# A transformer stack on one core: the rotation layer's QR and sign LU moved from TensorE and VectorE to row steps on GpSimd

## The chip, the cores and the metric

The kernel runs on one core of a Trainium2 chip. The metric is device time in microseconds for one launch, the median of three runs. The engines are named as in the profile: PE is TensorE (PEld its weight loads), DVE is VectorE, ACT is ScalarE, POOL is GpSimd, and SP is the queue that issues most DMAs. Each engine works through its own instructions strictly in the order of the program; semaphores tie the engines together.

## What is computed

Two images of 512 tokens with 144 channels pass through three transformer layers, each of 16 heads of width 9 with attention and an MLP of width 576 (layer 0 has four experts, two chosen per token). A last layer rotates the channels. Its matrices come from the weights and the condition alone:

```python
def _rotation(cond, W, b):
    v = jax.nn.silu(cond) @ W.T + b              # W: 2016 x 144
    A = zeros((2, 64, 64)); A[upper] = v; A[lower] = -v
    return expm(A)
U, _ = jnp.linalg.qr(P)                          # P: 144 x 64
R = _rotation(cond, W, b)
z = x @ U
x_rot = x + (z @ R - z) @ U.T
```

So beside the layers there is a solver: the entries v, the exponential of a 64 x 64 skew matrix for each image, and a QR of P, whose signs are fixed by an LU without pivoting of the upper 64 x 64 square of Q.

## The kernel before, in words

The layers run as 6 blocks (layer by image). A block is 64 steps, one for each head and each 128 keys; a step computes a tile of scores on PE, its exponential on ACT, and the row maxima of a later head (PE into one of three PSUM banks m_bank, then a reduce to row_max on DVE). Everything else is woven between the 384 steps: norms, the next block's q, k, v, the output projection, gates and MLPs of the block before. Which step a piece stands in comes from a table worked out when the kernel is built, and every engine walks the same table, each issuing its own part. POOL's parts are the norm's scale and shift (h_tok, L589 to L593), the low halves of q and k (L607, L609), and the split of each weight matrix into high and low halves (prep, L559 to L566, three layers and twelve MLPs). SP loads item after item of weights: one load waits until POOL has split the item before it.

The solver has three chains in the same table. The v chain takes steps 1 to 33 on DVE (L1051) and ends with a store to a DRAM scratch, from which SP fills the skew matrix with 63 small DMAs (L490). The exponential takes steps 141 to 257. The QR chain is the one that changes: 64 rounds "mgs" (modified Gram-Schmidt) and 64 rounds "lu". One round of either: PE spreads row j over 64 partitions by a matmul with a column of the identity (L1466, into an m_bank), DVE computes a coefficient for each row, and DVE adds the scaled row to all later rows (mgs: L1066 to L1079; lu: L1092 to L1101). 15 rounds lie in the head, before step 0; the others follow every two and a half steps, up to step 285, where signs, then y and m, make the final matrices.

```python
for i, part in enumerate(QR_CHAIN[EARLY:]):
    plan[i * QR_PACE // 2].append(part)
```

Of the kernel before, what the change touches and what calls it, by code (L numbers as in the profile page):

```python
# [26 lines left out]
ALU = mybir.AluOpType  # L27
# [4 lines left out]
P = 128  # L32
# [34 lines left out]
WCH = 2  # L67
# [79 lines left out]
QR_CHAIN = [("p_load",)] + [("mgs", j) for j in range(S)] + [("unit_cols",)]  # L147
QR_CHAIN += [("lu", j) for j in range(S)] + [("signs",), ("less_one",), ("y",), ("m", 0), ("m", 1)]
# [5 lines left out]
HEAD_SLOTS = sum(len(BANKS_OF[st[0]]) for st in HEAD)  # L154
EARLY = HEAD_SLOTS - HEAD_FROM + T * GRP // 2
QR_PACE = 5
# [20 lines left out]
def head_parts(slot):  # L177

    return QR_CHAIN[slot - HEAD_FROM:slot - HEAD_FROM + 1] if slot >= HEAD_FROM else []


def first_parts(i):

    at = HEAD_SLOTS - HEAD_FROM + i // 2
    return QR_CHAIN[at:at + 1] if i % 2 else []

SOLVER_BANK = ("v_rows", "p_load", "mgs", "lu", "skew", "taylor", "turned", "square", "y", "m")
# [46 lines left out]
def build(nc, a, out):  # L236
    with ExitStack() as ctx:
# [6 lines left out]
        def sem(name):  # L244
# [64 lines left out]
        w_rows = sb("w_rows", [VP, 2, WCH, C])  # L309
# [7 lines left out]
        bc_row = sb("bc_row", [S, C])  # L317
        bc_sq = sb("bc_sq", [S, C])
# [37 lines left out]
        w_in = [sem(f"w_in{i}") for i in range(2)]  # L356
# [7 lines left out]
                 "dve_done pool_done solver_full col_done v_summed "  # L364
# [65 lines left out]
        def _(sp):  # L430
# [17 lines left out]
            def load_w(i):  # L448
                if i >= 2:
                    sp.wait_ge(s["v_summed"], WCH * (i - 1))  # L450
                sp.dma_start(w_rows[:, i % 2, :, :],
                             a["L3_cond_W"].rearrange("(t p) c -> p t c", p=VP)[:, WCH * i:WCH * (i + 1), :])\
                    .then_inc(w_in[i % 2], 16)
# [22 lines left out]
            load_w(1)  # L476
            load_ada(1)
            load_item(1)
            for i in range(2, VT // WCH):
                load_w(i)  # L480
            load_item(2)
            load_item(3)

            sp.wait_ge(scratch_in, 16)
            sp.wait_ge(s["consts_ready"], 1)
            flat = v_scratch.rearrange("(b t) p -> b (t p)", b=B)
            off = 0
# [19 lines left out]
        def _(pool):  # L507
# [142 lines left out]
        def _(act):  # L650
# [87 lines left out]
            def solver(step):  # L738
# [19 lines left out]
            for i in range(T * GRP):  # L758
                mring.take()
                for part in first_parts(i):  # L760
                    solver(part)
# [24 lines left out]
        def _(dve):  # L786
# [248 lines left out]
            def solver(step, taken):  # L1035
# [10 lines left out]
                if kind == "v":  # L1046
                    t = step[1]
                    i = t // WCH
                    dve.wait_ge(w_in[i % 2], 16 * (i // 2 + 1))
                    for b in range(B):  # L1050
                        ins = dve.tensor_tensor_reduce(out=bc_scr[0:VP, :], in0=w_rows[:, i % 2, t % WCH, :],  # L1051
# [10 lines left out]
                elif kind == "mgs":  # L1062
                    j = step[1]
                    row = bk[0:S, 0:C]
                    dve.wait_ge(s["solver_full"], full)
                    link(dve.tensor_copy(bc_row[:, :], row))  # L1066
                    dve.tensor_tensor_reduce(out=bc_sq[:, :], in0=bc_row[:, :], in1=bc_row[:, :], scale=1.0, scalar=0.0,
                                             op0=ALU.mult, op1=ALU.add, accum_out=s_small[:, 3:4])\
                        .then_inc(s["dve_done"], 1)
                    dve.tensor_tensor_reduce(out=bc_scr[0:S, :], in0=q_rows[:, :], in1=bc_row[:, :], scale=1.0,  # L1070
                                             scalar=0.0, op0=ALU.mult, op1=ALU.add, accum_out=s_small[:, 0:1])\
                        .then_inc(s["dve_done"], 1)
                    done[0] += 2
                    fill[0]()
                    dve.wait_ge(s["dve_done"], done[0])
                    link(dve.reciprocal(s_small[:, 1:2], s_small[:, 3:4]))
                    link(dve.tensor_scalar(s_small[:, 2:3], s_small[:, 0:1], s_small[:, 1:2], neg_after[:, j:j + 1],
                                           ALU.mult, ALU.mult))
                    drain(dve.scalar_tensor_tensor(out=q_rows[:, :], in0=bc_row[:, :], scalar=s_small[:, 2:3],  # L1079
                                                   in1=q_rows[:, :], op0=ALU.mult, op1=ALU.add))  # L1080
                elif kind == "unit_cols":
                    link(dve.tensor_tensor_reduce(out=bc_scr[0:S, :], in0=q_rows[:, :], in1=q_rows[:, :], scale=1.0,
                                                  scalar=0.0, op0=ALU.mult, op1=ALU.add,
                                                  accum_out=s_small[:, 0:1]))
                    rsqrt(s_small[:, 1:2], s_small[:, 0:1], s_small[:, 2:3])
                    link(dve.tensor_scalar(q_rows[:, :], q_rows[:, :], s_small[:, 1:2], None, ALU.mult))
                    dve.tensor_copy(lu[:, :], q_rows[:, 0:S]).then_inc(s["col_done"], 1)
                elif kind == "lu":
                    j = step[1]
                    dve.wait_ge(s["solver_full"], full)  # L1090
                    w = bk[0:S, j:j + 1]
                    link(dve.tensor_scalar(s_sign[:, j:j + 1], w, 0.0, 2.0, ALU.is_ge, ALU.mult))  # L1092
# [89 lines left out]
            for i in range(T * GRP):  # L1182
                take_max(0, *divmod(i, GRP))
                for part in first_parts(i):
                    solve(part)
# [37 lines left out]
        def _(pe):  # L1223
# [221 lines left out]
            def solver(step):  # L1445
# [9 lines left out]
                elif kind == "p_load":  # L1455
                    pe.wait_ge(p_in, 64)
                    pe.transpose(bk[0:S, 0:P], p_nat[:, :], ident[:, :])
                    ins = pe.transpose(bk[0:S, P:C], p_nat_d[:, :], ident[0:CR, 0:CR])
                elif kind in ("mgs", "lu"):
                    j = step[1]  # L1460
                    src = q_rows[:, :] if kind == "mgs" else lu[:, :]
                    if kind == "lu" and j == 0:
                        pe.wait_ge(s["col_done"], 1)
                    else:
                        pe.wait_ge(*last[chain])
                    ins = pe.matmul(bk[0:S, 0:src.shape[1]], ident[0:S, j:j + 1].to_broadcast([S, S]), src,  # L1466
                                    start=True, stop=True)
# [48 lines left out]
            for i in range(T * GRP):  # L1516
                max_scores(0, *divmod(i, GRP))
                for part in first_parts(i):
                    solver(part)
# [40 lines left out]
```

## Time and profile before

| | us |
|---|---|
| median of 3 runs (lowest, highest) | 1165.92 (1162.24, 1166.27) |
| span of the profiled execution | 1173.7 |
| PE busy in it | 948.9 (81%) |
| DVE busy in it | 713.6 (61%) |
| ACT busy in it | 412.4 (35%) |
| POOL busy in it | 198.5 (17%) |

The profile is of one execution; the time of that execution is its span, 7.8 us above the median of the runs. Busy time counts work alone; an engine that waits for a semaphore is idle. Lines such as L1466 are lines of the kernel before. A line of a group of instructions has the shape "line engine operation out<-in, shapes, xcount | busy us, mean ns | idle us just before them and what ended it".

### The profile page before, as it was taken

Reading aid. Unit: us, or ns where it says so; the run is one execution under the profiler, and the core shown is the slowest. Engines: PE = TensorE matmul, PEld = TensorE weight load, DVE = VectorE, ACT = ScalarE, POOL = GpSimd, SP = SyncE. Lnnn points to the kernel's source line nnn. Section 1 sums busy time; section 2 is a strip of 40 time slices with the busy share of each in tenths; the row PEclk is TensorE's granted clock in tenths of the full one; section 3 lists DMA queues with packets and bytes.
Section 4 is the critical chain, followed back from the end, with each engine's and each line's share of the span. In section 5 each row is a group of like instructions: output and inputs, shape, how many; then the busy total and the mean of one; then the engine's idle time right before and its main releaser. Section 6 shows DMA issues by size and latency. Waiting matters only on the chain.

```text
span 1173.7 us, 12067 instructions
## 1 busy us (share of the span) xinstructions
PE 948.9 (81%) x3791; PEld 513.7 (44%) x3791; DVE 713.6 (61%) x2140; ACT 412.4 (35%) x742; POOL 198.5 (17%) x350
## 2 busy tenths in 40 slices
PE   4666889877898768889877788778887978989847
PEld 1432443335765433357644434535433534335326
DVE  4388767775353887772457767656677365564333
ACT  0302342324341333343424432415332436435412
POOL 5201014010240110042420000311002211012020
PEclk9999755556775655566866555657555656558556
DMA  3000001010111000001110000100000100000000
GB/s 101 13 1 10 16 6 43 1 29 1 29 29 29 17 1 1 1 16 42 34 38 0 1 1 1 29 1 1 1 1 0 30 0 1 1 1 1 6 5 11
DMA packets 22025, 16.01 MB, mean 14 GB/s; under 512 B 6427, under 2 KB 19391, under 8 KB 21962
## 3 DMA queue, kind: packets, MB, share of 16 engines
q1 hardware_dynamic: 21914, 15.22, 4.8%
q8 instruction: 31, 0.51, 0.2%
q14 instruction: 32, 0.26, 0.1%
q10 hardware_dynamic: 48, 0.02, 0.0%
HBM read 14.62 MB, written 0.61 MB: 13 GB/s over the span
## 4 chain that ended last, share of the span: by engine, by line
PE 61%; DVE 29%; issue 4%; ACT 4%; POOL 2%; DMA 0%; DVEq 0%; SPq 0%; ACTq 0%; POOLq 0%
PE o_bank L1289 11%; PE m_bank L1268 11%; DVE row_max L823 7%; PE s_bank L1257 3%; PE m_bank L1466 3%; PE d_bank L1350 3%; PE d_bank L1407 2%; PE d_bank L1409 2%; PE d_bank L1408 2%; PE m_bank L1276 2%; PE d_bank L1306 2%; PE d_bank L1307 2%; PE d_bank L1239 2%; PE d_bank L1392 2%; PE d_bank L1321 2%
## 5 line engine op out<-in xcount | busy, mean ns | idle before, releaser
L663 ACT ACTIVATE probs<-s_bank 128x512 f32<-128x512 f32 x384 | 220.4, 596 | 546.6 <-PE s_bank L1257 544.0
L823 DVE TENSOR_REDUCE row_max<-m_bank 128x1 fp32r<-128x512 f32 x384 | 256.0, 686 | 151.9 <-PE m_bank L1268 147.1
L1268 PE MATMUL m_bank<-k_t,q_t 32*128 32x512 f32 x384 | 216.5, 752 | 61.9 <-DVE q_rows L1079 24.2
L1257 PE MATMUL s_bank<-q_t,k_t 32*128 32x512 f32 x384 | 239.4, 749 | 5.8 <-ACT probs L663 4.9
L1289 PE MATMUL o_bank<-probs,v_aug 128*32 128x512 f32 x768 | 178.2, 1019 | 3.9 <-DVE o_tok L841 3.2
L1268 PEld LDWEIGHTS m_bank<-k_t,q_t 32*128 32x128 f32 x384 | 81.6, 271 | 181.9 <-issue 62.9
L1257 PEld LDWEIGHTS s_bank<-q_t,k_t 32*128 32x128 f32 x384 | 90.6, 272 | 30.9 <-ACT probs L663 16.1
L589 POOL TENSOR_TENSOR h_tok<-h_tok,mod 128x144 f32<-128x144 f32 x48 | 24.0, 499 | 297.3 <-DVE h_tok L882 297.3
L1407 PE MATMUL d_bank<-ff_hi,g_hi 128*128 128x144 f32 x192 | 60.7, 316 | 1.5 <-ACT g_hi L733 1.4
L1409 PE MATMUL d_bank<-ff_lo,g_hi 128*128 128x144 f32 x192 | 60.7, 316 | 0.0
L1408 PE MATMUL d_bank<-ff_hi,g_lo 128*128 128x144 f32 x192 | 60.5, 315 | 0.0
L1466 PE MATMUL m_bank<-q_rows,ident 64*64 64x144 f32 x128 | 45.9, 460 | 16.8 <-DVE q_rows L1079 16.8
L982 DVE TENSOR_TENSOR g_lo<-g_raw,g_hi 128x512 fp32r<-128x512 f32 x48 | 37.3, 787 | 34.1 <-ACT g_hi L733 33.9
L1321 PE MATMUL d_bank<-ident,h_tok 128*128 128x128 f32 x80 | 35.0, 439 | 19.4 <-POOL h_tok L593 19.4
L607 POOL TENSOR_TENSOR qs_tok<-qkv_tok,qs_tok 128x144 fp32r<-128x144 f32 x24 | 12.0, 500 | 222.9 <-ACT ks_tok L712 222.9
L1276 PEld LDWEIGHTS m_bank<-ident_r,row_max 128*128 128x128 f32 x96 | 22.3, 323 | 62.3 <-issue 39.0
L592 POOL COPY h_tok<-o_tok 128x144 f32<-128x144 f32 x24 | 7.4, 307 | 245.0 <-DVE o_tok L841 215.2
L1392 PE MATMUL d_bank<-h_hi,ff_hi 128*128 128x512 f32 x60 | 33.1, 552 | 19.1 <-ACT g_hi L733 12.6
L731 ACT ACTIVATE g_raw<-d_bank 128x512 f32<-128x512 f32 x60 | 36.0, 600 | 31.2 <-PE d_bank L1395 23.9
L1407 PEld LDWEIGHTS d_bank<-ff_hi,g_hi 128*128 128x128 f32 x192 | 44.1, 230 | 4.9 <-ACT g_hi L733 4.9
L1276 PE MATMUL m_bank<-ident_r,row_max 128*128 128x128 f32 x96 | 26.6, 429 | 24.1 <-DVE q_rows L1079 9.1
L1409 PEld LDWEIGHTS d_bank<-ff_lo,g_hi 128*128 128x128 f32 x192 | 44.7, 233 | 0.0
(232 smaller groups left out, 1639.4 us busy)
## 6 DMA issues: line engine op xcount, KB each, us to landing
raw_a<-in_L_cond_w_dram SPq DMA_DIRECT2D x20, 288.0 KB
raw_a<-in_L_cond_W_fc_dram SPq DMA_DIRECT2D x4, 288.0 KB
w_rows<-in_L_cond_W_dram SPq DMA_DIRECT2D x8, 141.8 KB
raw_d<-in_L_cond_w_dram SPq DMA_DIRECT2D x30, 36.0 KB
raw_a<-in_L_cond_w_dram SPq DMA_DIRECT2D x20, 36.0 KB
x_tok<-in_x_dram SPq DMA_DIRECT2D x2, 288.0 KB, 4.2
out_dram<-moe SPq DMA_DIRECT2D x4, 144.0 KB, 1.9
raw_d<-in_L_cond_w_dram SPq DMA_DIRECT2D x30, 4.0 KB
```

The costliest lines, as they stand in the source:

```text
L663: act.activation(probs[:, n % PROBS, :], s_banks[n % S_BANKS][:, :], ACT.Exp, scale=HD ** -0.5)\
L823: dve.tensor_reduce(row_max[:, grp % 2, t, MAXROW + 32 * j:MAXROW + 32 * j + 1], bk[:, :], AX.X, ALU.max).then_inc(drained, 1)
L1257: pe.matmul(s_banks[n % S_BANKS][:, :], k_t[rows, par, g, kt * P:(kt + 1) * P], q_t[rows, par, g, :], start=True, stop=True).then_inc(s["s ...
L1268: pe.matmul(bk[:, :], q_t[rows, par, g, t * P:(t + 1) * P], k_t[rows, par, g, :], start=True, stop=True).then_inc(s["max_full"], 1)
L1276: ins = pe.matmul(bk[:, t * P:(t + 1) * P], row_max[:, grp % 2, t, :], ident_r[:, :], start=True, stop=True)
L1289: ins = pe.matmul(o_bank[32 * j:32 * j + 32, :], v_aug[:, par, kt, at:at + 32], probs[:, (GRP * quad + j) % PROBS, :], start=(kt == 0), st ...
L1321: pe.transpose(a_bank[:, cols], h_tok[:, t, 0:P], ident[:, :])
L1392: pe.matmul(bk[:, :], ff_hi[:, i, c], h_hi[:, :], start=True, stop=False)
L1407: pe.matmul(dst, g_hi[:, f, cols], ff_hi[:, i, w], start=(f == 0), stop=False)
L1408: pe.matmul(dst, g_lo[:, f, cols], ff_hi[:, i, w], start=False, stop=False)
L1409: pe.matmul(dst, g_hi[:, f, cols], ff_lo[:, i, w], start=False, stop=False)
L1466: ins = pe.matmul(bk[0:S, 0:src.shape[1]], ident[0:S, j:j + 1].to_broadcast([S, S]), src, start=True, stop=True)
```

## The change

The QR becomes an elimination on the Gram matrix: the head computes P'P and the transposed P side by side as one tile aug of 64 x 208, and 63 rounds "gs" on POOL clear it row by row; the 64 lu rounds go to POOL too. In each round SP sends the pivot row to all 64 partitions by a DMA from SBUF to SBUF (row_out), and POOL waits for it, works out the coefficient (the reciprocal is a power of minus one), scales the row and adds it. A round stands at every second step from step 0 on; the rounds in the head are gone. Since SP now sends rows, its whole list is written along the steps: rows, weight items, the four loads of the v chain (of four tiles each, into a single buffer where two of two tiles took turns) and the 63 skew DMAs each stand where their step is. DVE waits for all 63 gs at step 126 (unit_cols) and for the last lu at step 256 (signs).

```diff
-WCH = 2
+WCH = 4
-QR_PACE = 5
+QR_PACE = 2
-    for i, part in enumerate(QR_CHAIN[EARLY:]):
-        plan[i * QR_PACE // 2].append(part)
+    for i, part in enumerate(QR_CHAIN):
+        plan[i * QR_PACE].append(part)
...
+            def row_out(k):
+                kind, j = SWEEPS[k]
+                if k == 0:
+                    sp.wait_ge(m_drained[0], 1)
+                elif k == S - 1:
+                    sp.wait_ge(s["col_done"], 1)
+                else:
+                    sp.wait_ge(s["swept"], k)
+                src = (aug if kind == "gs" else lu)[j:j + 1, j:]
+                w = src.shape[1]
+                sp.dma_start(row_bc[:, j:j + w], src.unsqueeze(1).to_broadcast([1, S, w]))\
+                    .then_inc(row_in, 16)
...
+            for n in range(BLOCKS * STEPS):
+                for i in range(2, ITEMS):
+                    if PREP_AT[i - 1] == n:
+                        load_item(i)
+                for part in SOLVER_PLAN[n]:
+                    if part[0] == "v" and part[1] % WCH == WCH - 1 and part[1] < VT - 1:
+                        load_w(part[1] // WCH + 1)
+                    if part in SWEEPS and part != SWEEPS[-1]:
+                        row_out(SWEEPS.index(part) + 1)
+                    if part[0] == "v_rows":
+                        sp.wait_ge(scratch_in, 16)
...
+                pool.wait_ge(row_in, 16 * (k + 1))
+                if step[0] == "gs":
+                    link(pool.tensor_tensor(inv, row, minus_one[:, :], ALU.pow))
+                    link(pool.tensor_scalar(coef, rows[:, j:j + 1], inv, after, ALU.mult, ALU.mult))
+                else:
+                    link(pool.tensor_scalar(s_sign[:, j:j + 1], row, 0.0, 2.0, ALU.is_ge, ALU.mult))
...
+                    link(pool.tensor_scalar(piv, s_sign[:, j:j + 1], -1.0, row, ALU.add, ALU.add))
+                    link(pool.tensor_tensor(sq, piv, piv, ALU.mult))
+                    link(pool.tensor_tensor(inv, sq, minus_one[:, :], ALU.pow))
+                    link(pool.tensor_scalar(inv, inv, piv, after, ALU.mult, ALU.mult))
+                    link(pool.tensor_scalar(coef, rows[:, j:j + 1], inv, None, ALU.mult))
+                link(pool.tensor_scalar(row_bc[:, rest], row_bc[:, rest], coef, None, ALU.mult))
+                pool.tensor_tensor(rows[:, rest], rows[:, rest], row_bc[:, rest], ALU.add).then_inc(s["swept"], 1)
```

Three places of the order matter below. The first is SP where the v chain ends. Before, the skew DMAs (L490) followed the loads of weight items 2 and 3 in SP's list:

```order
L437 DMA raw_a<-in_L_cond_w_proj_dram 128x144
L437 DMA raw_d<-in_L_cond_w_proj_dram 16x144 x3
L437 DMA raw_d<-in_L_cond_b_proj_dram 1x144 x2
L490 DMA skew<-v_scratch 1x2x63 [waits consts_ready,scratch_in]
L490 DMA skew<-v_scratch 1x2x62
L490 DMA skew<-v_scratch 1x2x61
```

Now, on SP, they stand (as L522) behind the DMA of row 17, which is the row of 191 columns (a row of gs(j) has 208 - j columns):

```order
L477 DMA row_bc<-aug 64x1x193 [waits swept]
L477 DMA row_bc<-aug 64x1x192 [waits swept]
L477 DMA row_bc<-aug 64x1x191 [waits swept]
L522 DMA skew<-v_scratch 1x2x63 [waits consts_ready,scratch_in]
L522 DMA skew<-v_scratch 1x2x62
L522 DMA skew<-v_scratch 1x2x61
```

Behind the last of the 63, still on SP, come rows 18 to 22 and the load of weight item 2, which waits for POOL's split of item 1:

```order
L522 DMA skew<-v_scratch 1x2x2
L522 DMA skew<-v_scratch 1x2x1
L477 DMA row_bc<-aug 64x1x190 [waits swept]
L477 DMA row_bc<-aug 64x1x189 [waits swept]
L477 DMA row_bc<-aug 64x1x188 [waits swept]
L477 DMA row_bc<-aug 64x1x187 [waits swept]
L477 DMA row_bc<-aug 64x1x186 [waits swept]
L448 DMA raw_a<-in_L_cond_w_dram 128x576 [waits weights_ready]
```

So all 63 skew DMAs now lie between rows 17 and 18, and the items lie behind row 22. The second place is POOL before its norm of block 0 (h_tok from o_tok). Before, the three splits (ff for items 1 and 2, lay for item 3) followed the last low half of k directly:

```order
L609 TENSOR_TENSOR ks_tok<-qkv_tok,ks_tok 128x16x9
L559 CAST ff_hi<-raw_a 128x1360 [waits item_in]
L560 TENSOR_TENSOR ff_lo<-raw_a,ff_hi 128x1360 [waits pool_done]
L564 CAST ff_d<-raw_d 96x784
L566 TENSOR_TENSOR ff_d<-raw_d,ff_d 32x784 [waits pool_done]
L559 CAST ff_hi<-raw_a 128x1360 [waits item_in,weights_ready]
L560 TENSOR_TENSOR ff_lo<-raw_a,ff_hi 128x1360 [waits pool_done]
```

Now POOL has gs rounds in front of them (this is gs(20), gs(21) and the split of item 1):

```order
L665 TENSOR_TENSOR pivot<-row_bc,minus_one 64x1 [waits row_in]
L666 TENSOR_SCALAR pivot<-aug,pivot,neg_after 64x1 [waits pool_done]
L677 TENSOR_SCALAR row_bc<-row_bc,pivot 64x187 [waits pool_done]
L678 TENSOR_TENSOR aug<-aug,row_bc 64x187 [waits pool_done]
L665 TENSOR_TENSOR pivot<-row_bc,minus_one 64x1 [waits row_in]
L666 TENSOR_SCALAR pivot<-aug,pivot,neg_after 64x1 [waits pool_done]
L677 TENSOR_SCALAR row_bc<-row_bc,pivot 64x186 [waits pool_done]
L678 TENSOR_TENSOR aug<-aug,row_bc 64x186 [waits pool_done]
L589 CAST ff_hi<-raw_a 128x1360 [waits item_in]
```

Each split and each h_tok now stands behind every gs round of an earlier step. The third place is PE in the steps of block 0, where before a solver matmul (L1466) stood between scores and maxima and waited for banks that DVE empties:

```order
L1268 MATMUL m_bank<-k_t,q_t 128x512 [waits m_drained2]
L1257 MATMUL s_bank<-q_t,k_t 128x512 [waits probs_ready]
L1466 MATMUL m_bank<-q_rows,ident 64x144 [waits m_drained0]
L1268 MATMUL m_bank<-k_t,q_t 128x512 [waits m_drained1]
L1257 MATMUL s_bank<-q_t,k_t 128x512 [waits probs_ready]
```

Now, on PE, only the maxima (L1283) use these banks there, beside the scores (L1272) and o_bank:

```order
L1283 MATMUL m_bank<-k_t,q_t 128x512 [waits m_drained0]
L1272 MATMUL s_bank<-q_t,k_t 128x512 [waits probs_ready]
L1304 MATMUL o_bank<-probs,v_aug 32x512 [waits probs_ready]
L1304 MATMUL o_bank<-probs,v_aug 32x512 x3
L1283 MATMUL m_bank<-k_t,q_t 128x512 [waits m_drained1]
L1272 MATMUL s_bank<-q_t,k_t 128x512 [waits probs_ready]
```

The 128 solver matmuls are gone from PE, and with them their turns in the ring of three banks.

## Rows read from the trace of the kernel before

**Rows 1.** The page: the chain that ended last, shares of the span.

```profile
PE 61%; DVE 29%; issue 4%; ACT 4%; POOL 2%; DMA 0%; DVEq 0%; SPq 0%; ACTq 0%; POOLq 0%
```

**Rows 2.** Groups by line on PE: the solver's matmul and the maxima behind it.

```profile
L1268 PE MATMUL m_bank<-k_t,q_t 32*128 32x512 f32 x384 | 216.5, 752 | 61.9 <-DVE q_rows L1079 24.2 <-DVE lu L1101 16.5 <-DVE row_max L823 14.6
...
L1466 PE MATMUL m_bank<-q_rows,ident 64*64 64x144 f32 x128 | 45.9, 460 | 16.8 <-DVE q_rows L1079 16.8
```

**Rows 3.** Timeline of DVE before step 0 (start, length): pairs of maxima, four rounds apart.

```profile
63.13 1.29 DVE L823 TENSOR_REDUCE row_max<-m_bank 128x1 fp32r<-128x512 f32 x2
...
75.06 1.29 DVE L823 TENSOR_REDUCE row_max<-m_bank 128x1 fp32r<-128x512 f32 x2
```

**Rows 4.** Timeline of POOL: starts of h_tok, image 1, then block 0.

```profile
94.85 0.53 POOL L589 TENSOR_TENSOR h_tok<-h_tok,mod 128x144 f32<-128x144 f32 x1 [36.38 <-DVE h_tok L882]
...
238.14 0.30 POOL L592 COPY h_tok<-o_tok 128x144 f32<-128x144 f32 x1 [29.87 <-issue]
```

**Rows 5.** Groups by line on POOL: two long operations, two short ones.

```profile
L560 POOL TENSOR_TENSOR ff_lo<-raw_a,ff_hi 128x1360 fp32r<-128x1360 f32 x12 | 37.3, 3106 | 7.8 <-issue 6.9
...
L590 POOL TENSOR_TENSOR h_tok<-h_tok,mod 128x144 f32<-128x144 f32 x48 | 23.7, 494 | 3.8
...
L593 POOL COPY h_tok<-h_tok 128x32 f32<-128x32 f32 x80 | 16.7, 213 | 50.2 <-DVE h_tok L880 45.7
L559 POOL CAST ff_hi<-raw_a 128x1360 fp32r<-128x1360 f32 x12 | 16.0, 1330 | 112.3 <-PE d_bank L1417 103.9 <-DMA raw_d<-in_L_cond_b_dram 8.4
```

**Rows 6.** DMA issues: KB each, then us from issue to landing.

```profile
x_tok<-in_x_dram SPq DMA_DIRECT2D x2, 288.0 KB, 4.2
...
c_row<-in_cond_dram SPq DMA_DIRECT2D x1, 144.0 KB, 3.1
...
p_nat_d<-in_L_cond_P_dram SPq DMA_DIRECT2D x1, 4.0 KB, 1.6
qk_gain<-in_L_cond_g_q_dram SPq DMA_DIRECT2D x1, 4.5 KB, 2.3
qk_gain<-in_L_cond_g_k_dram SPq DMA_DIRECT2D x1, 4.5 KB, 2.6
...
v_scratch<-v_row ACTq DMA_DIRECT2D x1, 15.8 KB, 1.4
```

**Rows 7.** Timeline of POOL: splits of items 1 (start) and 3 (start, last operation).

```profile
173.75 1.39 POOL L559 CAST ff_hi<-raw_a 128x1360 fp32r<-128x1360 f32 x1
...
204.04 0.66 POOL L559 CAST lay_hi<-raw_a 128x576 fp32r<-128x576 f32 x1 [7.32 <-DMA raw_d<-in_L_cond_b_proj_dram]
...
206.87 1.40 POOL L566 TENSOR_TENSOR lay_d<-raw_d,lay_d 32x576 fp32r<-32x576 f32 x1
```

**Rows 8.** Timeline of SP: first issue of item 3, then the skew DMAs.

```profile
196.75 0.35 SPq L437 DMA_DIRECT2D raw_a<-in_L_cond_w_qkv_dram  x1
...
201.94 36.63 SPq L490 DMA_DIRECT2D skew<-v_scratch  x63
```

**Rows 9.** Busy time of L1466 by stretch: stretch, length, PE and PEld busy (count), clock, DMA.

```profile
238.00:387.00 149.00, 7.81 (x22) 3.04 (x22) 0.64 0.10 26
387.00:478.00 91.00, 8.90 (x28) 3.89 (x28) 0.54 0.00 1
478.00:611.00 133.00, 4.28 (x20) 2.55 (x20) 0.68 0.11 29
611.00:709.00 98.00, 7.38 (x32) 4.46 (x32) 0.53 0.00 1
709.00:787.00 78.00, 3.59 (x16) 2.18 (x16) 0.59 0.04 11
787.00:879.00 92.00, 7.08 (x34) 4.35 (x34) 0.59 0.00 1
879.00:1173.70 294.70, 4.29 (x20) 2.57 (x18) 0.60 0.02 5
```

**Rows 10.** Groups by line on PE from 879.00 us to the end.

```profile
L1466 PE MATMUL m_bank<-lu,ident 64*64 64x64 f32 x20 | 4.6, 334 | 11.1 <-DVE lu L1101 11.1
```

More of the change, by code:

```diff
@@ L146 @@
 V_CHAIN = [("v", t) for t in range(VT)] + [("v_rows",)]
-QR_CHAIN = [("p_load",)] + [("mgs", j) for j in range(S)] + [("unit_cols",)]
-QR_CHAIN += [("lu", j) for j in range(S)] + [("signs",), ("less_one",), ("y",), ("m", 0), ("m", 1)]
+SWEEPS = [("gs", j) for j in range(S - 1)] + [("lu", j) for j in range(S)]
+QR_CHAIN = SWEEPS[:S - 1] + [("unit_cols",)] + SWEEPS[S - 1:]
+QR_CHAIN += [("signs",), ("less_one",), ("y",), ("m", 0), ("m", 1)]
 EXP_CHAIN = [("skew",), ("scale",)] + [("taylor", n) for n in range(TAYLOR - 1, 0, -1)] + [("turned",)]
@@ L177, in head_parts, with prep_steps @@
 def head_parts(slot):
[L179 to L189, printed above, removed]
+    return [("p_load",)] if slot == HEAD_FROM else []
+def prep_steps():
+    at, slots = {}, [n for n in range(BLOCKS * STEPS) for _ in range(SLOTS[n])] + [BLOCKS * STEPS] * 8
+    slot = 0
+    for st in WOVEN:
+        if st[0] == "prep":
+            at[st[1]] = slots[slot]
+        if st[0] == "mlp" and 1 <= st[1] < MLPS - 1:
+            at[mlp_item(st[1] + 1)] = slots[slot]
+        slot += len(ROOM[st[0]])
+    return at
+PREP_AT = prep_steps()
+SOLVER_BANK = ("v_rows", "p_load", "skew", "taylor", "turned", "square", "y", "m")
 MAX_SHARE = [2, 2] + [1] * (GSTEPS - 4) + [0, 0]
@@ L307, in build @@
         ident_r = sb("ident_r", [P, P], F32R)
-        w_rows = sb("w_rows", [VP, 2, WCH, C])
+        w_rows = sb("w_rows", [VP, WCH, C])
         v_col = sb("v_col", [VP, B, VT])
@@ L355, in build @@
         p_in = sem("p_in")
-        w_in = [sem(f"w_in{i}") for i in range(2)]
+        w_in = sem("w_in")
+        row_in = sem("row_in")
         scratch_in = sem("scratch_in")
@@ L626, in solver @@
                     pool.partition_all_reduce(rs_norm[:, 1, :], rs_norm[:, 0, :], S, RMAX).then_inc(s["norm_out"], 1)
+                if step not in SWEEPS:
+                    return
+                j, k = step[1], SWEEPS.index(step)
+                row, rest = row_bc[:, j:j + 1], slice(j + 1, (S + C) if step[0] == "gs" else S)
+                rows, after = (aug if step[0] == "gs" else lu), neg_after[:, j:j + 1]
+                piv, inv, coef, sq = (pivot[:, i:i + 1] for i in range(4))
+                pool.wait_ge(row_in, 16 * (k + 1))
[4 more added lines that the diff above has]
+                    link(pool.tensor_scalar(s_sign[:, j:j + 1], row, 0.0, 2.0, ALU.is_ge, ALU.mult))
+                    if j == S - 1:
+                        pool.tensor_copy(lu[:, j:j + 1], row).then_inc(s["swept"], 1)
+                        return
+                    link(pool.tensor_scalar(piv, s_sign[:, j:j + 1], -1.0, row, ALU.add, ALU.add))
[5 more added lines that the diff above has]
+                pool.tensor_tensor(rows[:, rest], rows[:, rest], row_bc[:, rest], ALU.add).then_inc(s["swept"], 1)
             walk = {"norm": norm, "qkv": qkv, "mlp": mlp}
@@ L1061, in solver @@
                     dve.tensor_tensor(v_row[:, :], bk[0:B * VT, 0:VP], vb_row[:, :], ALU.add).then_inc(drained, 1)
[L1062 to L1080, printed above, removed]
@@ L1456, in solver @@
                     pe.wait_ge(p_in, 64)
[L1457 to L1467, printed above, removed]
+                    pe.matmul(bk[0:S, 0:S], p_nat[:, :], p_nat[:, :], start=True, stop=False)
+                    pe.matmul(bk[0:S, 0:S], p_nat_d[:, :], p_nat_d[:, :], start=False, stop=True)
+                    pe.transpose(bk[0:S, S:S + P], p_nat[:, :], ident[:, :])
+                    ins = pe.transpose(bk[0:S, S + P:S + C], p_nat_d[:, :], ident[0:CR, 0:CR])
                 elif kind == "skew":
```

85 lines of the change are left out of this document (30 added, 55 removed).

## The prediction

> **What bounds the kernel now.** I read first the chain of the work that ended last, [rows 1]: 61% of the span is PE, 29% DVE, and POOL 2%. The groups by line then say what the QR has to do with that. A maxima matmul (L1268) waited 24.2 us for a DVE that was finishing an mgs round and 16.5 us for one finishing a lu round, and the solver's own matmul (L1466) 16.8 us for the round before it [rows 2]: 57.5 us in which PE stood still for the QR, beside its busy time, which the stretches give as 43.3 us after 238 us [rows 9]. So the QR does lie on the path. The timeline of POOL shows the other side: an engine that waits most of the time, but whose norms PE waits for. 238.1 us is where h_tok of block 0 begins [rows 4], and POOL had been idle 29.87 us before it.
>
> **What the change removes.** Ahead of step 0, eight mgs rounds stood between the maxima. Two pairs of maxima four rounds apart are 11.93 us apart [rows 3], 2.98 for a round with its maxima; without the round the pair of maxima takes 1.29. That saves 1.69 a round, 13.5 us for eight. The seven rounds in the head I count at nothing: they lie between loads and turns, and 7 x 1.69 = 11.8 us is the most that they can hold. After 238 us I credit L1466's busy time in each stretch [rows 9], and the 11.1 us that it waited in the last stretch [rows 10] by half (5.6), since a DVE that was behind there may be behind with other work. The other waits on DVE's rounds stay out of the sum; they are the unknown on the side of a gain.
>
> **What a round costs now.** The trace has no such operation on POOL, so I fit two lines to [rows 5]. Two inputs: (3106 - 494) / (1360 - 144) = 2.15 ns a column, 185 ns at no width. One input: (1330 - 213) / (1360 - 32) = 0.84 ns, 186 ns at no width. L590 shows 3.8 / 48 = 0.08 us between dependent operations. A gs round has four: pow and coefficient on one column (an estimate of 0.25 each; 0.19 is the lower bound, 0.5 for pow alone my upper one), the scaled row, some 190 wide, 0.35, the addition 0.59, gaps 0.32: 1.8 us. A lu round has eight, narrower: five at 0.19, pow 0.25, 0.21, 0.25, gaps 0.64: 2.3 us.
>
> The row's DMA is the disputed price. No DMA of the trace has SBUF at both ends. The nearest [rows 6]: plain 4 KB 1.6 us, a store out of SBUF 1.4, 4.5 KB spread over 128 partitions 2.3 and 2.6, 144 KB spread likewise 3.1. For gs I take the mean of 1.6, 2.3, 2.6 and 3.1, 2.4 us; for the shorter lu rows that of the first three, 2.2; bounds 1.6 and 3.1. With 0.1 us from POOL's semaphore to SP (an estimate) a gs round takes 1.8 + 0.1 + 2.4 = **4.3 us**, a lu round 2.3 + 0.1 + 2.2 = **4.6**. Nothing overlaps within a round: row k+1 leaves only when sweep k is over.
>
> **Stage A, to h_tok of block 0.** Image 1's h_tok is twelve operations of 0.53, 0.494 and 0.213 (four of each), 5.0 us, from 94.85 [rows 4, 5]; gs(0) begins at 94.85 + 5.0 - 13.5 = 86.4 us. gs(16) is over at 86.4 + 16 x 4.3 + 1.8 = 157.0. Three rows (those behind rows 4, 8 and 12) queue behind a load of w_rows; x_tok, of the same size, took 4.2 us [rows 6], so each is late by 4.2 - 2.4 = 1.8, together 5.4: 162.4. Row 17 leaves, and now SP issues the 63 skew DMAs: 36.6 us in the trace of before [rows 8], where nothing waited behind them but weights. Now rows 18 and on do: 199.0, and row 18 is there at 201.5. (The v chain itself should be done by then; its last loads go with row 12, at some 142.) gs(18) to gs(21): 3 x 4.3 + 1.8, 216.2. Then POOL splits items 1 and 2, with the load between them, which before took from 173.75 to the first issue of item 3 at 196.75 [rows 7, 8], 23.0: 239.2. SP issues item 3, 201.94 - 196.75 = 5.2: 244.4; row 23 lands 2.5 later, 246.9. gs(23) to gs(33), 10 x 4.3 + 1.8: 291.7. The split of item 3, 208.27 - 204.04 = 4.2 [rows 7]: 295.9. Only then h_tok of block 0 comes, for which PE waits in step 70: **57.8 us later** than 238.1. DVE and ACT reach that step early and wait too, so what was saved before the step is lost there.
>
> **Stages after it** [rows 9]. In each stretch the longer of two paths decides: PE's (the stretch less L1466), or POOL's (h_tok 5.0, then its rounds one behind the other).
> 238 to 387: four rounds fit into what the weights leave; -7.8, lag 50.0.
> 387 to 478: POOL 5.0 + 15 x 4.3 + 3 (unit_cols on DVE, an estimate) + 2 x 4.6 = 81.7, PE 91 - 8.9 = 82.1; -8.9, 41.1.
> 478 to 611: -4.3, 36.8.
> 611 to 709: POOL 5.0 + 19 x 4.6 = 92.4, above PE's 90.6; 98 before, -5.6, 31.2.
> 709 to 787: -3.6, 27.6.
> 787 to 879: POOL 92.4 + 3 for the signs on DVE = 95.4 against 92; +3.4, 31.0.
> To the end: -4.3 - 5.6, 21.1.
> The profiled execution took 1173.7, so its counterpart takes 1194.8; the median lies 7.8 below such an execution: **1187 us**, 1.8% slower.
>
> **Rivals.** Half a per cent, 6 us, is about what a measurement of this kernel can tell.
>
> *The row lands as a plain small load (faster).* At 1.6 us (the 4 KB load and the store speak for it, and that the broadcasts stood among many loads [rows 6]) a gs round takes 3.5 and a lu round 4.0. Stage A: 86.4 + 16 x 3.5 + 1.8 + 3 x 2.6 = 152.0; + 36.6 + 1.7 = 190.3; + 10.5 + 1.8 + 23.0 + 5.2 + 1.7 = 232.5; + 35 + 1.8 + 4.2 = 273.5, a lag of 35.4. POOL then holds nobody up in the later stretches, and all of L1466 and its last wait come back: 43.3 + 11.1 = 54.4. 1173.7 + 35.4 - 54.4 - 7.8 = **1147 us**, less if the other waits of [rows 2] vanish too. The gs round decides: from 4.3 down, each 0.1 us takes 2.6 us from stage A and up to 1.9 from each lu stretch; the 21 us are paid back near a round of 3.9. Chance 0.27.
>
> *The row is dear and so is pow (slower still).* At 3.1 us, with pow at 0.5, a gs round takes 5.25, a lu round (2.6) 5.25 too. For it: all 64 receivers read one source row, as in c_row, and pow is no operation of before. Stage A + 29 x 0.95 - 3 x 0.7 = 25.5 more; the three POOL paths become 5.0 + 15 x 5.25 + 3 + 10.5 = 97.3 (against 91), 104.8 (98) and 107.8 (92), in place of -8.9, -5.6 and +3.4: +15.2, +12.4, +12.4. 1187 + 65.5 = **1252 us**. Chance 0.20.
>
> A page bears on that rival. The Trainium skill, "SBUF — State Buffer", section "Door 1: The DMA port swizzle", says that four neighbouring partitions share one port, through which it measured 27.6 GB/s. By that, an estimate from its figure, 64 reads of one row of 190 floats (49 KB) would take 1.8 us more than a row from many partitions, and the time would come out at this rival's or above. No run here shows a source in SBUF so far.
>
> *No change.* A round near 3.9 us: lag and relief cancel, 1160 to 1172. Chance 0.08. The forecast itself (1165 to 1220, which laps over that case's end) has 0.45.
>
> **The numbers.** Faster is the first rival and the forecast's thin lower edge: 0.28; same 0.10; slower 0.62. The range leaves out what lies under 1133 (first rival with all waits gone) and the upper half of the second rival: 1133 to 1252.
>
> **What would show it.** On SP, a gap of about 37 us between rows 17 and 18, and POOL idle before gs(18); h_tok of block 0 on POOL near 296 us; PE idle before it for tens of us in step 70; POOL's wait for row_in at the pow, 2.5 us a round, and the landing of row_bc. DVE should wait at unit_cols and at signs by a few us only, and the waits of L1268 on q_rows and lu be gone. I am wrong if rows land in under 2 us, if the 63 issues take less than 30 us when rows stand behind them, if pow takes a us, or if PE's idle time before the maxima stays (then DVE, not the QR, set it).

## The result, and the profile after

The changed kernel takes 1290.11 us (median of 4 runs, 1288.64 to 1292.76) against 1164.53 for the kernel before: a ratio of 1.1085, with a 95% interval of 1.1042 to 1.1127. The forecast was 1187 us with a range of 1133 to 1252. The sign was right; the size was not, and the time lies outside the range. Here and below a time is the median of all runs of a kernel, and a ratio is taken over its faster runs alone, those within 1.5% of its fastest.

The page of the kernel after, with the busy times and the chain that ended last, answers to [rows 1]:

```profile
PE 854.8 (66%) x3539; PEld 456.9 (35%) x3539; DVE 553.5 (43%) x1308; ACT 409.1 (32%) x742; POOL 512.0 (40%) x1109
...
PE 29%; POOL 26%; DMA 19%; DVE 10%; issue 7%; SPq 5%; ACT 3%; DVEq 0%; POOLq 0%; ACTq 0%
```

PE and DVE have lost 94 and 160 us of work, as the change meant. The chain shows what took their place: before, POOL held 2% of it and DMA nothing; now POOL, DMA and SP's queue hold half.

The waits of the whole kernel after (who waited for whom, total, times, longest):

```profile
POOL pivot L665 <- DMA row_bc<-aug: 208.1, 52, 35.1
...
PE d_bank L1336 <- POOL h_tok L623: 174.5, 21, 107.5
...
POOL s_sign L668 <- DMA row_bc<-lu: 103.1, 49, 5.7
```

The 107.5 us is one wait. Timeline of PE around it, with h_tok of block 0 on POOL, which answers to the second row of [rows 4]:

```profile
231.32 0.79 PE L1272 MATMUL s_bank<-q_t,k_t 32*128 32x512 f32 x1
339.64 0.45 PE L1336 MATMUL d_bank<-ident,h_tok 128*128 128x128 f32 x1 [107.53 <-POOL h_tok L623]
```

```profile
338.92 0.30 POOL L622 COPY h_tok<-o_tok 128x144 f32<-128x144 f32 x1
```

PE was through with its work ahead of the transposes of h_tok at 232.1, 6 us before the same norm even began in the kernel before, and then stood still. What stood in front of the norm is on SP and POOL. Timeline of SP (start, length), which answers to [rows 8]:

```profile
158.41 24.37 SPq L477 DMA_DIRECT2D row_bc<-aug  x5
182.91 37.03 SPq L522 DMA_DIRECT2D skew<-v_scratch  x63
219.99 24.37 SPq L477 DMA_DIRECT2D row_bc<-aug  x5
```

Timeline of POOL: all of gs(17) and the first operation of gs(18), with the idle time before it in brackets:

```profile
185.75 0.56 POOL L665 TENSOR_TENSOR pivot<-row_bc,minus_one 64x1 f32<-64x1 f32 x1 [2.59 <-DMA row_bc<-aug]
186.42 0.33 POOL L666 TENSOR_SCALAR pivot<-aug,pivot,neg_after 64x1 f32<-64x1 f32 x1
186.84 0.77 POOL L677 TENSOR_SCALAR row_bc<-row_bc,pivot 64x190 f32<-64x190 f32 x1
187.70 0.59 POOL L678 TENSOR_TENSOR aug<-aug,row_bc 64x190 f32<-64x190 f32 x1
223.44 0.57 POOL L665 TENSOR_TENSOR pivot<-row_bc,minus_one 64x1 f32<-64x1 f32 x1 [35.15 <-DMA row_bc<-aug]
```

The gap of 37 us between rows 17 and 18 is there. Elsewhere a gs round, from one power to the next, takes 5.98 us (median of the 62 distances between starts of L665) and a lu round 5.4.

DMA issues of the kernel after (KB, us to landing), widest and narrowest gs row and the widest lu row:

```profile
row_bc<-aug SPq DMA_DIRECT2D x1, 52.0 KB, 3.5
...
row_bc<-aug SPq DMA_DIRECT2D x1, 36.5 KB, 2.9
...
row_bc<-lu SPq DMA_DIRECT2D x1, 16.0 KB, 2.1
```

From 16.0 to 52.0 KB the landing grows by 1.4 us: 36 KB in 1.4 us, some 26 GB/s, on top of about 1.5 us at no width (an estimate from the same three rows).

The stretches of the kernel after, cut at the same h_tok marks as [rows 9] (the length, then busy time and number of all instructions of PE, PEld, DVE, ACT and POOL, then the granted clock, the DMA share and GB/s):

```profile
338.90:459.20 120.30, 99.41 (x484) 65.12 (x484) 58.83 (x138) 47.23 (x78) 59.00 (x84) 0.76 0.18 33
459.20:567.10 107.90, 60.45 (x236) 27.29 (x236) 56.54 (x142) 35.67 (x69) 47.76 (x101) 0.55 0.09 6
567.10:715.50 148.40, 112.81 (x491) 74.12 (x491) 61.18 (x152) 47.26 (x77) 81.67 (x147) 0.64 0.12 30
715.50:825.90 110.40, 71.45 (x287) 33.96 (x287) 58.43 (x142) 37.50 (x71) 58.87 (x172) 0.53 0.01 2
825.90:897.70 71.80, 59.87 (x246) 32.60 (x246) 40.97 (x99) 21.69 (x36) 43.92 (x113) 0.57 0.05 13
897.70:1003.00 105.30, 73.13 (x326) 37.88 (x326) 48.16 (x94) 36.26 (x70) 53.64 (x168) 0.55 0.01 1
1003.00:1288.50 285.50, 231.94 (x994) 121.00 (x992) 135.41 (x302) 115.32 (x208) 43.20 (x96) 0.61 0.02 6
```

Against the kernel before (149, 91, 133, 98, 78, 92, 295) the attention stretches, where POOL has its rounds in a row, are 12 to 17 us longer, and the MLP stretches shorter but for the third row.

DVE waits for the rounds too, and PE then waits for the maxima that DVE still owes it. From the waits of the kernel after (the first line is to be held against the 14.6 us of [rows 2]):

```profile
PE m_bank L1283 <- DVE row_max L873: 102.6, 17, 26.8
...
DVE bc_scr L1100 <- DMA w_rows<-in_L_cond_W_dram: 46.4, 3, 20.9
...
DVE bc_scr L1113 <- POOL aug L678: 24.3, 1, 24.3
...
DVE bc_scr L1121 <- POOL lu L670: 17.3, 1, 17.3
```

L1100 is the v chain, whose loads now stand behind rows in SP's list and go into a single buffer (no run tells the two apart); L1113 is unit_cols and L1121 is signs.

### The profile page after: what moved, and what is told of

The parts are those of the page before. It is cut to its first block, busy times and chain, and to the rows that moved or that the text cites. A ratio compares the mean times of both kernels' runs of the same rounds, so it can differ in the third digit from the quotient of the medians.

```text
span 1288.5 us, 11367 instructions
## 1 busy us (share of the span) xinstructions
PE 854.8 (66%) x3539; PEld 456.9 (35%) x3539; DVE 553.5 (43%) x1308; ACT 409.1 (32%) x742; POOL 512.0 (40%) x1109
## 4 chain that ended last, share of the span: by engine, by line
PE 29%; POOL 26%; DMA 19%; DVE 10%; issue 7%; SPq 5%; ACT 3%; DVEq 0%; POOLq 0%; ACTq 0%
DMA row_bc<-aug 11%; DMA row_bc<-lu 7%; PE o_bank L1304 5%; POOL row_bc L677 5%; PE m_bank L1283 3%; SPq L522 3%; POOL pivot L674 2%; DVE row_max L873 2%; POOL pivot L665 2%; POOL aug L678 2%; SPq L448 2%; PE d_bank L1422 2%; PE s_bank L1272 2%; PE d_bank L1424 2%; PE d_bank L1423 2%
## 5 line engine op out<-in xcount | busy, mean ns | idle before, releaser
L873 DVE TENSOR_REDUCE row_max<-m_bank 128x1 fp32r<-128x512 f32 x384 | 248.5, 685 | 391.7 <-PE m_bank L1283 387.5
L1283 PE MATMUL m_bank<-k_t,q_t 32*128 32x512 f32 x384 | 193.8, 745 | 109.8 <-DVE row_max L873 102.6
L1272 PE MATMUL s_bank<-q_t,k_t 32*128 32x512 f32 x384 | 224.0, 750 | 15.6 <-ACT probs L715 10.2
L1283 PEld LDWEIGHTS m_bank<-k_t,q_t 32*128 32x128 f32 x384 | 72.9, 272 | 230.4 <-DVE row_max L873 127.0
L665 POOL TENSOR_TENSOR pivot<-row_bc,minus_one 64x1 f32<-64x1 f32 x63 | 36.6, 581 | 208.4 <-DMA row_bc<-aug 208.1
L1272 PEld LDWEIGHTS s_bank<-q_t,k_t 32*128 32x128 f32 x384 | 83.6, 271 | 57.5 <-ACT probs L715 32.6
L1336 PEld LDWEIGHTS d_bank<-ident,h_tok 128*128 128x128 f32 x80 | 15.3, 191 | 201.4 <-issue 185.6
L677 POOL TENSOR_SCALAR row_bc<-row_bc,pivot 64x207 f32<-64x207 f32 (+62 forms) x126 | 73.1, 580 | 12.1
L668 POOL TENSOR_SCALAR s_sign<-row_bc 64x1 f32<-64x1 f32 x64 | 16.8, 263 | 110.7 <-DMA row_bc<-lu 103.1
L1422 PE MATMUL d_bank<-ff_hi,g_hi 128*128 128x144 f32 x192 | 55.5, 289 | 3.3 <-DVE g_lo L1032 1.6
L1365 PE MATMUL d_bank<-ident_r,qs_tok 128*128 128x128 f32 x96 | 25.3, 412 | 47.7 <-POOL ks_tok L639 47.5
L1407 PE MATMUL d_bank<-h_hi,ff_hi 128*128 128x512 f32 x60 | 33.8, 564 | 30.3 <-DVE logits L999 15.1
L1365 PEld LDWEIGHTS d_bank<-ident_r,qs_tok 128*128 128x128 f32 x96 | 21.5, 311 | 63.4 <-issue 63.4
L1422 PEld LDWEIGHTS d_bank<-ff_hi,g_hi 128*128 128x128 f32 x192 | 38.6, 201 | 7.9 <-ACT g_hi L785 5.7
```

Source lines behind the costliest of these rows:

```text
L665: link(pool.tensor_tensor(inv, row, minus_one[:, :], ALU.pow))
L677: link(pool.tensor_scalar(row_bc[:, rest], row_bc[:, rest], coef, None, ALU.mult))
L873: dve.tensor_reduce(row_max[:, grp % 2, t, MAXROW + 32 * j:MAXROW + 32 * j + 1], bk[:, :], AX.X, ALU.max).then_inc(drained, 1)
L1272: pe.matmul(s_banks[n % S_BANKS][:, :], k_t[rows, par, g, kt * P:(kt + 1) * P], q_t[rows, par, g, :], start=True, stop=True).then_inc(s["s ...
L1283: pe.matmul(bk[:, :], q_t[rows, par, g, t * P:(t + 1) * P], k_t[rows, par, g, :], start=True, stop=True).then_inc(s["max_full"], 1)
L1336: pe.transpose(a_bank[:, cols], h_tok[:, t, 0:P], ident[:, :])
```

## The experiments

**Spread the skew DMAs.** In SP's list the 63 DMAs no longer follow row 17 in one piece:

```diff
 if part in SWEEPS and part != SWEEPS[-1]:
     row_out(SWEEPS.index(part) + 1)
+    for _ in range(2):
+        if todo:
+            skew_row(todo.pop(0))
...
```

> The changed kernel with the 63 skew DMAs no longer in one piece behind row 17: two of them follow each later row. Theory A (SP's 37 us in one piece delay gs(18) and with it h_tok of block 0): h_tok of block 0 begins 37 us earlier, near 302 us instead of 338.9, and the time falls from 1290 to some 1253. Rival B (the lag is POOL's rounds and splits alone, SP's piece lies beside other waits): h_tok stays near 339 and the time at 1285 to 1290. Part of the gain can be lost if a stage further on waits for the same rounds; then 1255 to 1275.

1267.53 us; ratio 1.0839 (1.0695 to 1.0983), against 1.1085 without it. h_tok of block 0 begins at 309.6 us, 29 earlier. Theory A holds with a smaller sum: the piece costs its 37 us less about one round, since row 17 was under way beside it. The four runs spread from 1248.6 to 1274.5 us, so the time saved (16 to 41 us) is known less well than the start of h_tok; the two runs with cheap rounds, below, are the cleaner pair for the same edit.

**Each partition its own row.** The same bytes, but from 64 partitions:

```diff
-src = (aug if kind == "gs" else lu)[j:j + 1, j:]
-sp.dma_start(row_bc[:, j:j + w], src.unsqueeze(1).to_broadcast([1, S, w]))
+src = (aug if kind == "gs" else lu)[:, j:]
+sp.dma_start(row_bc[:, j:j + w], src)
...
```

> The changed kernel with every partition fed from its own row of aug or lu in place of row j: same bytes, same number of issues, but the reads leave 64 partitions and not one (the elimination is left out, neg_after is made tiny so that values stay finite). Theory A (the 64 reads of one source partition queue at it; the landing of 3.45 us at 52 KB and 2.9 at 36.5 KB is a fixed part of some 1.5 us and 26 GB/s): the row lands in 1.5 to 2.0 us at every width, a gs round takes 4.3 to 4.6 us in place of 6.1, and the time falls to 1195 to 1215. Rival B (the landing is a matter of the bytes or of the broadcast's 64 descriptors as such): 3.4 us stays and the time stays at 1285 to 1290.

1213.97 us, ratio 1.0466 (1.0368 to 1.0564). Its DMA issues (KB, us to landing), to be held against those of the kernel after:

```profile
row_bc<-aug SPq DMA_DIRECT2D x1, 52.0 KB, 1.9
...
row_bc<-aug SPq DMA_DIRECT2D x1, 36.5 KB, 1.8
...
row_bc<-lu SPq DMA_DIRECT2D x1, 16.0 KB, 1.7
```

The page's line of the DMA queue that carries nearly all packets (packets, MB, the time that the packets took as a share of 16 engines' span), of the kernel after and then of this run:

```profile
q1 hardware_dynamic: 32018, 18.62, 8.5%
```

```profile
q1 hardware_dynamic: 32018, 18.62, 6.0%
```

The dependence on the bytes is almost gone, with the same bytes, the same number of packets and the same 64 destinations; the packets themselves took less time. So what cost 1.6 us at full width is that all reads leave one partition; the gs round falls to 4.53 us, as theory A has it.

**Products for the powers.**

```diff
-link(pool.tensor_tensor(inv, row, minus_one[:, :], ALU.pow))
+link(pool.tensor_tensor(inv, row, minus_one[:, :], ALU.mult))
-link(pool.tensor_tensor(inv, sq, minus_one[:, :], ALU.pow))
+link(pool.tensor_tensor(inv, sq, minus_one[:, :], ALU.mult))
...
```

> The changed kernel with the two powers of minus one made products (no reciprocal is computed; neg_after is made tiny so that values stay finite). Theory A (POOL's operations lie in the serial round, and a power takes 0.58 us): the operation takes 0.2 us, each of 126 rounds is 0.38 us shorter, h_tok of block 0 comes 33 x 0.38 = 12.5 us earlier, and the whole is 30 to 45 us faster, 1245 to 1260. Rival B (rounds are paced by the steps, not by their own length, outside block 0): only the 12.5 us of block 0, 1278.

1249.38 us, ratio 1.0768 (1.0682 to 1.0853): 41 us less, for 126 powers that are 0.37 and 0.39 us shorter each (47 us). Groups by line on POOL of the kernel after, then of this run, the power of a gs and of a lu round:

```profile
L674 POOL TENSOR_TENSOR pivot<-pivot,minus_one 64x1 f32<-64x1 f32 x63 | 36.7, 582 | 4.9
L665 POOL TENSOR_TENSOR pivot<-row_bc,minus_one 64x1 f32<-64x1 f32 x63 | 36.6, 581 | 208.4 <-DMA row_bc<-aug 208.1
```

```profile
L665 POOL TENSOR_TENSOR pivot<-row_bc,minus_one 64x1 f32<-64x1 f32 x63 | 13.3, 212 | 209.6 <-DMA row_bc<-aug 209.3
...
L674 POOL TENSOR_TENSOR pivot<-pivot,minus_one 64x1 f32<-64x1 f32 x63 | 12.1, 192 | 4.9
```

Nearly all of what a round loses comes back in the time. So the rounds are the path in most of the program, not only ahead of block 0's norm.

**Both, as a round of the predicted length.** The two edits above together.

> The changed kernel with both costs of the round taken down together: rows read from 64 partitions (each its own row) and products in place of the powers; elimination and reciprocals are left out, every issue, wait and order stays. A gs round should take 4.1 to 4.2 us and a lu round 4.7 to 4.8, about the 4.3 and 4.6 of the prediction. Theory A (the prediction's chain of waits was right and only the two round lengths were mis-sized): its sum for such rounds, 1187 us, holds to 12 us: 1175 to 1199, and h_tok of block 0 begins at 285 to 296 us. Rival B (there is another loss of the moved rounds that the sum lacks): 1205 or more.

1177.96 us, ratio 1.0141 (1.0045 to 1.0238). The rounds take 4.15 and 4.71 us, and h_tok of block 0 begins at 285.2:

```profile
285.19 0.30 POOL L622 COPY h_tok<-o_tok 128x144 f32<-128x144 f32 x1
```

Given the lengths, the prediction's sum holds to 9 us, as theory A has it. Its terms hold less well. Three stretches of this run, the first MLP stretch, the first attention stretch with rounds in a row, and the MLP stretch behind it:

```profile
285.19:401.55 116.36, 98.73 (x484) 64.23 (x484) 59.40 (x138) 47.24 (x78) 55.51 (x85) 0.76 0.12 34
401.55:492.99 91.44, 54.90 (x236) 25.66 (x236) 55.72 (x142) 35.77 (x69) 40.98 (x100) 0.61 0.03 7
492.99:634.24 141.25, 113.25 (x491) 74.99 (x491) 65.00 (x152) 47.25 (x77) 76.67 (x146) 0.66 0.12 32
```

Against the kernel before they are 32 us shorter, as long, and 8 us longer, where the prediction has 7.8 shorter, 8.9 shorter and 4.3 shorter. Part of the agreement in the sum is luck: errors of both signs cancel.

**Both, and the skew DMAs spread.**

> The same with the 63 skew DMAs spread, two behind each later row. Theory A (lag of block 0 is the rounds, the splits and SP's 37 us less a round): h_tok of block 0 begins some 30 us earlier than in the run with cheap rounds alone, 255 to 265 us, the time is 20 to 30 us lower, 1148 to 1172, about that of the kernel before. Rival B (with shorter rounds the v chain or the loads take the place of the skew DMAs): less than 12 us between the two.

1147.23 us, ratio 0.9845 (0.9757 to 0.9934): 31 us less than the run before, with h_tok 32.8 us earlier. It lies a us below the expected band, as theory A has it; with rounds of 4.15 us and no piece on SP the moved order would be a gain of 1 to 2%, but this kernel computes no elimination, and no run has such a round that does.

```profile
252.36 0.30 POOL L626 COPY h_tok<-o_tok 128x144 f32<-128x144 f32 x1
```

**All rounds 55 steps later.**

```diff
-plan[i * QR_PACE].append(part)
+plan[55 + i * QR_PACE].append(part)
```

> The changed kernel with every QR part 55 steps later (gs(0) in step 55, m(1) in step 319), nothing else moved. Theory A (a norm pays for the rounds that stand in front of it on POOL, and nothing asks for the rounds themselves early): h_tok of block 0 has 7 rounds in front of it in place of 34, so it begins at 225 to 240 us in place of 338.9; the stretches after it stay POOL bound and the last one gets six to eight stages of rounds too (10 to 25 us); time 1195 to 1225. Rival B (the chain of 127 rounds itself, 127 x 5.8 us, has to fit ahead of its last part): starting 55 steps later gives nothing or costs, 1290 or more.

1230.35 us, ratio 1.0622 (1.0526 to 1.0718), 5 us above the band. The first half of theory A holds: with 7 rounds in front of it, h_tok of block 0 begins at 229.6 us, 109 earlier.

```profile
229.61 0.30 POOL L622 COPY h_tok<-o_tok 128x144 f32<-128x144 f32 x1
```

49 of the 109 us are given back: from that norm to the end this run takes 60 us more than the kernel before, where the kernel after takes 14 more, and the stretch from 914.9 us, which has rounds here and none in the kernel after, is 16 us longer than in the kernel before. Moving the rounds later moves much of the cost.

**Wider pace, skew DMAs spread.** gs at every 2.7 steps, lu at every 2.1 from step 173:

```diff
-plan[i * QR_PACE].append(part)
+plan[i * 27 // 10 if i < S else 173 + (i - S) * 21 // 10].append(part)
...
```

> The changed kernel with the skew DMAs spread as before in this study, and the rounds set wider: gs at every 2.7 steps, lu at every 2.1 from step 173, m(1) in step 317. Theory A (as above): h_tok of block 0 has 25 rounds in front of it in place of 34, begins near 255 to 270 us; the gs stretch behind it costs nothing (13.7 rounds of 5.8 us in 37 steps), lu stretches cost as now; 1185 to 1215. Rival B (SP's and POOL's lists hold PE up whatever the pace): within 15 us of the kernel with spread skew DMAs alone, 1250 to 1268.

1214.33 us, ratio 1.0482 (1.0388 to 1.0576), in theory A's band; h_tok of block 0 at 264.0. This is the fastest of the versions here that compute the whole QR on POOL, and it is still 5% slower than before.

**The elimination alone, on the engines of before.** One matmul spreads the row; on DVE:

```diff
...
+dve.reciprocal(s_small[:, 1:2], bk[0:S, 0:1])
+dve.tensor_scalar(s_small[:, 2:3], aug[:, j:j + 1], s_small[:, 1:2], neg_after[:, j:j + 1],
+                  ALU.mult, ALU.mult)
+dve.scalar_tensor_tensor(out=aug[:, j + 1:], in0=bk[0:S, 1:S + C - j], scalar=s_small[:, 2:3],
+                         in1=aug[:, j + 1:], op0=ALU.mult, op1=ALU.add)
...
```

> One part alone: the kernel before with the elimination on the Gram matrix in place of mgs, still on TensorE and VectorE (one matmul, then reciprocal, coefficient and one addition on DVE, 208 - j columns), lu as before, no row DMAs, SP's and POOL's lists as before. Theory A (the elimination is cheaper than mgs, 3 DVE operations of about 0.95 us in place of 6 of 1.83 us, and only the move to POOL and SP costs time): 1125 to 1155, faster than before. Rival B (wider rows eat what the fewer operations save, or the waits of PE stay): 1160 to 1170.

1124.26 us, ratio 0.9679 (0.9581 to 0.9776): 3.2% faster than the kernel before. Its three operations of a gs round on DVE, by line:

```profile
L1070 DVE SCALAR_TENSOR_TENSOR aug<-m_bank,s_small,aug 64x207 f32<-64x207 f32 (+62 forms) x63 | 24.7, 393 | 2.2
...
L1068 DVE TENSOR_SCALAR s_small<-aug,s_small,neg_after 64x1 f32<-64x1 f32 x63 | 16.4, 260 | 1.2 <-DVE s_small L1064 0.3
L1064 DVE RECIPROCAL s_small<-m_bank 64x1 f32<-64x1 f32 x63 | 9.9, 156 | 33.7 <-PE m_bank L1459 32.2 <-DVE q_t L829 0.4
```

That is 0.81 us of work on DVE in a round. The new algorithm is a gain; the loss comes with the new place and the order that goes with it.

**The elimination on DVE, lu on POOL.** SWEEPS holds only the lu rounds, one at every 2.75 steps:

```diff
-SWEEPS = [("gs", j) for j in range(S - 1)] + [("lu", j) for j in range(S)]
+SWEEPS = [("lu", j) for j in range(S)]
+QR_CHAIN = [("p_load",)] + [("gs", j) for j in range(S - 1)] + [("unit_cols",)] + SWEEPS
...
```

> The Gram elimination on TensorE and VectorE as in the run before that was faster, but the 64 lu rounds on POOL with rows by SP as in the change, one at every 2.75 steps from step 125 to 301. Theory A (POOL's rounds cost nothing where a round of 5.2 us has some 8 us of steps): no matmul and no DVE operation of lu is left on the path, DVE loses 63 us of work and PE its waits on lu; 1085 to 1112. Rival B (each norm and split of POOL behind such a round still waits for a DMA, and DVE was not what bound those stretches): 1120 to 1150, no better than with lu on DVE.

1123.14 us, ratio 0.9682 (0.9577 to 0.9787): no better than with lu on DVE, as rival B has it in its result, and no worse: at this wide pace the lu rounds on POOL cost nothing against DVE. One stretch, cut at the same two h_tok marks in the run with both on DVE and then in this one, shows one part of why:

```profile
903.28:968.44 65.16, 56.64 (x260) 26.96 (x260) 38.39 (x78) 36.53 (x72) 8.26 (x21) 0.67 0.00 1
```

```profile
889.61:968.27 78.66, 67.61 (x256) 32.37 (x256) 37.47 (x73) 35.20 (x69) 20.50 (x63) 0.52 0.00 1
```

Up to there, this run was 14 us ahead; here it loses them all. PE is 11 us longer busy with nearly the same number of instructions, at a granted clock of 0.52, almost all of it the lower of its two levels (1.2 of 2.4 GHz), in place of 0.67. So what was saved before was given back at the lower clock for the greater part; why the clock stayed low there was not tested, and B's own reason is not shown.

## Why the prediction was wrong

**The step that failed is "What a round costs now".** It put a gs round at 4.3 us and a lu round at 4.6; they take 5.98 and 5.4. For gs(17), with its row of 191 columns: the landing 3.4 against 2.4 (+1.0); the power 0.56 against 0.25 (+0.3); the coefficient 0.33 against 0.25 (+0.1); the scaled row 0.77 against 0.35 (+0.4); the addition 0.59 as worked out. The landing was an average over DMAs whose sources lie in DRAM. Sources in SBUF were in sight, in the store of [rows 6] (the prediction's word that no run shows one overlooks it), but no row of the kernel before had one partition of SBUF read 64 times; that cost 1.6 us at 52 KB. In a lu round it was the other way: the landing was right (2.1 against 2.2), and POOL's eight operations with their gaps take 3.3 us in place of 2.3.

The rule that was cited beside the second rival bears on this: the Trainium skill, "SBUF — State Buffer", section "Door 1: The DMA port swizzle", gives 27.6 GB/s, measured at 1 MiB, for four neighbouring partitions behind one port. The trace agrees with it in size: 26 GB/s, and 1.6 us less as soon as the reads leave 64 partitions, where the estimate from its figure was 1.8. Whether the port or the partition itself sets this rate is not shown; no run read from the neighbours alone.

The scaled row was costed by the wrong neighbour. The line for one input came from casts and copies (0.84 ns a column); L677, which scales with a scalar for each partition, goes from 659 ns at 145 columns to 835 at 207, 2.8 ns a column.

The second rival, "The row is dear and so is pow", had the right mechanisms, and still too small a price: 5.25 for a round, because its upper bound for the landing was again a row with a source in DRAM and it kept the cheap scaled row. Its 1252 us fell 38 short.

**Stage A was right in its links.** With measured lengths its chain reads: gs(0) at 82.6, gs(16) over at 182.3, SP's piece to 220.0, split of item 1 at 243.8, item 3's issue at 266.6, split of item 3 at 334.65, h_tok at 338.9. The prediction had 86.4, 162.4, 199.0, 216.2, 239.2, 291.7 and 295.9. The lag is 100.8 us in place of 57.8, 43.0 of the miss. One small term fell away: rows behind a load of w_rows landed in the usual 3.4 us, so the 5.4 us for them were not there.

**The stages after it** were to give back 36.7 us and cost 14.0 more, 50.7 of the miss. The three stretches counted as POOL's rounds in a row came out at +16.7, +12.9 and +13.2, where -8.9, -5.6 and +3.4 were forecast. In the run with cheap rounds they are +0.3, +4.0 and +4.3, so the round's length is the greater part of it and not the whole. The count was off as well: the sum has 4 gs rounds in the first MLP stretch and 15 in the attention stretch behind it, and 13 and 16 stand there.

What else it missed is DVE. It put the waits at unit_cols and at signs at a few us; they were 24.3 and 17.3, and PE stood 26.8 and 17.8 us before the maxima behind them. (With cheap rounds, 14.2 and 10.7 are left at DVE.) The MLP stretch from 567 us has +15.1 against -4.3, and part of that is a wait of the same kind. The exponential's norm is POOL's too (L656), and behind lu rounds DVE waited for it:

```profile
DVE sq_on L1141 <- POOL rs_norm L656: 16.0, 1, 16.0
```

I had named POOL's norms and splits as queued behind the rounds, and not this one. The run with cheap rounds still has 14.1 us of the same wait. On the other side the first MLP stretch gave 28.5 us, where 7.8 were forecast; the last section has what is known of that.

The last 9.4 us are the step from the profiled execution to the median: 7.8 below it was assumed, 1.6 above it was found. 43.0 + 50.7 + 9.4 = 103.1, the whole miss.

**What was right:** the sign, the place of the stall, the gap on SP, and that L1268's waits on q_rows and lu vanish. Its counterpart L1283 waits for other things all the same: its idle time is 109.8 us, 102.6 of them for row_max, against 61.9 of L1268. The prediction had named this as a sign of being wrong, with the reading that DVE, not the QR, set the time. That reading does not hold here: the longest of these waits stand behind DVE's own waits for w_rows, unit_cols and signs. Of the rivals, "The row lands as a plain small load" and "No change" are out: at full width 1.9 us was reached only by leaving the broadcast out.

## What to carry to other kernels

Before serial rounds are moved to an idle engine, work out one round to its last hop: the DMA's landing with its real source, every short operation, and what else stands in that engine's list behind the rounds. An engine that is 17% busy is not free when others wait for the rest of its work in order. Where both the algorithm and the engine change, try the new algorithm on the old engines first: here it is worth 3.2% there, and the move turned that into a loss of 11%. When a sum comes out right, look at its terms too: with cheap rounds this one did, and single stretches were off by up to 25 us.

## What was not expected of the hardware

A row that is read 64 times from one partition lands in 2.1 us at 16 KB and 3.5 at 52 KB, some 26 GB/s on top of 1.5 us; the same bytes from 64 partitions land in 1.7 and 1.9 us. A power on POOL takes 0.58 us on one column, a product 0.2.

TensorE's clock gave something back after the stall, though not at once: the granted clock was 0.5, the lower of its two levels (1.2 of 2.4 GHz), while PE stood still and also from 339.6 us, where PE began again, to 378; from 380 us to the end of the first MLP stretch it averages 0.89. Over the whole stretch it averages 0.76, with 0.64 in the same stretch before, and the 64 matmuls of L1422 take 281 ns each where those of L1407, the same line before, took 346 (the kernel after, then the kernel before):

```profile
L1422 PE MATMUL d_bank<-ff_hi,g_hi 128*128 128x144 f32 x64 | 18.0, 281 | 1.2 <-ACT g_hi L785 1.1
```

```profile
L1407 PE MATMUL d_bank<-ff_hi,g_hi 128*128 128x144 f32 x64 | 22.1, 346 | 0.0
```

PE had been idle for 107.5 us and ran the stretch with 27 us less of busy time, of which L1466's matmuls account for 7.8. That the idle time raised the clock is not shown: the run with both on DVE has 0.70 there without such a stall.
